# DLRM interaction and top layers on one core: the last two tables looked up whole, pairs in three chunks, layer 2's bias by a product, the sum's column turned by VectorE

## The chip, the cores and the metric

One of the cores of a Trainium2 chip runs the whole program. The metric is the device time of one execution in microseconds (us), lower is better. Engines in the text: TensorE (PE, with its weight loads as PEld), VectorE (DVE), ScalarE (ACT), GpSimd (POOL), SyncE (SP, which only issues transfers here).

## The reference

512 samples. Each has 26 embedding rows of 128 floats, picked by index out of 26 tables, and one dense row `r_bottom_output` of 128 floats. All 27 rows are multiplied with each other, and the 351 products of different rows go, with the dense row, through three layers:

```python
e = stack([tbl_f[ids[:, f]] for f in range(26)], axis=1)
all_emb = concatenate([bottom[:, None, :], e], axis=1)           # 512 x 27 x 128
gram = einsum('bfd,bgd->bfg', all_emb, all_emb)
z = gram[:, TRIU_I, TRIU_J]                                      # 512 x 351
h = concatenate([z, bottom], axis=1)                             # 512 x 479
h = maximum(h @ W_top1 + b_top1, 0)                              # 512 x 512
h = maximum(h @ W_top2 + b_top2, 0)                              # 512 x 256
y = h @ W_top3                                                   # 512 x 1
```

## The kernel before, in words

The samples stand in four tiles of 128 (`TILES`). Rows of 14 tables (`GATHERED`) come by indirect transfers that GpSimd issues, 56 of them, one for each tile and table (L348), and are turned on TensorE in four groups per tile, of 4, 4, 4 and 2 tables (step `turn`, L648), and copied to `emb` by ScalarE (L442). Rows of the other 12 tables (`LOOKED_UP`, each of 1000 or 1250 rows) are found by a product with a matrix of ones and zeros: VectorE writes `onehot` in 8 (for two tables 10) pieces of 128x512 (L518), ScalarE rounds the table to `hi`, VectorE takes the rest as `lo` (L501), and TensorE adds `hi` times `onehot` and `lo` times `onehot` (step `look`, L609), each in a first and a second half of the pieces.

The last two looked-up tables (numbers 10 and 11) are not looked up that way but in steps `part`: samples 0 to 255 first, samples 256 to 511 later, between the first `gram` steps, each with a moving operand of 256 columns (L636). ScalarE copies the sums of both tables to `emb` for each half of the samples (L434).

Behind that the steps of each tile t are: `gram` in four parts, each 32 small products (L671); VectorE and ScalarE copy one half of the products each to `gram` (L528, L451); VectorE turns them in 32x32 blocks in two instructions (L535, L536) and picks the 351 pairs to `z` (L543); `pairs`, TensorE turns `z` in three chunks of 117 (L679), ScalarE copies all three at once (L459) to `zt`; `bottom`, the dense part of layer 1 (L696), in two halves; `l1`, four steps of three products (L705), each step one block of 128 outputs over all chunks, and ScalarE's bias and maximum (L472); `l2` (L714), bias on VectorE (L549), and maximum, product with `W_top3` and sum in one instruction with a read of the accumulator (L551); `out`, a product with the identity turns the column of 128 sums into a row (L720), ScalarE copies it (L477), SP stores it (L328), in three stores for tiles 0, 1, and 2 and 3.

All engines run through one hand-written list, `ORDER` (L95 to L121), each doing its own share of a step; so a step's place in the list sets what every engine queues ahead of it. `turn`, `pairs`, `l2` and `out` share two PSUM banks (`ring`, `BANKS` = 2) in turn: a step waits on TensorE until the step two before it in that list has been copied out (`wait_emptied`, L556). `gram` uses three banks of `acc`, layer 1 three others. The products in f32 are two instructions each on TensorE; the rows count instructions.

## Time and profile before

| | |
|---|---|
| median of 3 runs | 107.57 us (107.38 to 110.34) |
| the profiled execution | 107.59 us |
| its span, first to last instruction | 105.9 us |
| TensorE busy | 98.3 us (93%), granted clock 0.999 |
| VectorE busy | 67.9 us (64%) |
| ScalarE busy | 53.2 us (50%) |
| GpSimd busy | 60.3 us (57%) |

The span is 1.7 us shorter than the execution's own time; what the change does is worked out inside the span and taken off the execution's time. "Busy" of TensorE is no measure of how fast it goes: instructions overlap, and the pace of a step is best read from start to start, or in the chain of work that ended last, where each piece is counted once.

### The profile page before, as it was taken

The numbers are of one execution on the slowest core, as the hardware profiler recorded it, in microseconds if no ns is written. First come the engines' busy times: TensorE is split into PE (matmuls) and PEld (weight loads), VectorE is DVE, ScalarE is ACT, GpSimd is POOL, SyncE is SP. The second block draws the span as 40 slices with busy tenths as digits, with TensorE's granted clock in tenths as the row PEclk, the third lists the DMA queues.
The fourth block names the chain that finished last, engine by engine and source line by source line (L and its number), as shares of the span: only waits on it lengthen the run. The fifth ranks groups of instructions, "written<-read, shape, count | busy, mean of one in ns | idle before, by whom it ended". The sixth has DMA issues, their size and how long they took to land.

```text
span 105.9 us, 3533 instructions
## 1 busy us (share of the span) xinstructions
PE 98.3 (93%) x1506; PEld 82.3 (78%) x1506; DVE 67.9 (64%) x157; ACT 53.2 (50%) x89; POOL 60.3 (57%) x65
## 2 busy tenths in 40 slices
PE   4999999999999999999769989999999989999971
PEld 4777777888888888888659979889888977996850
DVE  5499999999999999999940019108330833094021
ACT  3497659719939986984421324343153324222220
POOL 3777778877778877787777777777770000000000
PEclk9999999999999999999999999999999999999999
DMA  3899999658866845112699321222220000000000
GB/s 52 300 351 291 283 305 214 239 141 280 237 168 233 220 89 205 50 50 64 186 293 299 86 57 50 62 68 53 59 56 25 6 6 0 6 3 0 6 0 0
DMA packets 7460, 13.48 MB, mean 127 GB/s; under 512 B 1734, under 2 KB 3881, under 8 KB 7444
## 3 DMA queue, kind: packets, MB, share of 16 engines
q1 hardware_dynamic: 5340, 9.05, 28.0%
q0 software_dynamic: 1792, 3.67, 14.1%
q10 hardware_dynamic: 312, 0.52, 1.4%
q8 instruction: 12, 0.20, 0.7%
q14 instruction: 4, 0.03, 0.2%
HBM read 13.23 MB, written 0.01 MB: 125 GB/s over the span
## 4 chain that ended last, share of the span: by engine, by line
PE 47%; DVE 41%; issue 8%; ACT 1%; POOL 1%; POOLq 0%; DVEq 0%; ACTq 0%
DVE onehot L518 29%; PE acc L705 12%; PE acc L671 11%; DVE lo L501 11%; PE ring L714 7%; PE acc L636 6%; PE acc L696 4%; PE ring L648 3%; PE ring L679 2%; PE acc L573 2%; PE ring L720 1%; PE acc L587 1%; ACT far L379 1%; ACT zt L459 0%; DVE h L549 0%
## 5 line engine op out<-in xcount | busy, mean ns | idle before, releaser
L348 POOL DMA_INDIRECT rows<-tbl,ids_sb x56 | 59.5, 1062 | 18.3 <-issue 16.8
L518 DVE TENSOR_SCALAR onehot<-far 128x512 fp32r<-128x512 f32 x83 | 31.6, 437 | 1.3 <-ACT far L379 1.3
L609 PE MATMUL acc<-onehot,hi 128*128 128x512 f32 x84 | 23.8, 407 | 0.2 <-DVE onehot L518 0.2
L609 PE MATMUL acc<-onehot,lo 128*128 128x512 f32 x84 | 22.7, 393 | 0.0
L609 PEld LDWEIGHTS acc<-onehot,lo 128*128 128x128 f32 x84 | 15.8, 188 | 3.6
L609 PEld LDWEIGHTS acc<-onehot,hi 128*128 128x128 f32 x84 | 15.0, 191 | 4.3 <-DVE onehot L518 1.7
L528 DVE COPY gram<-acc 128x432 f32<-128x432 f32 x4 | 3.7, 917 | 22.3 <-PE acc L671 22.3
L365 ACT CAST hi<-raw 128x1024 fp32r<-128x1024 f32 (+1 forms) x11 | 12.0, 1088 | 10.7 <-issue 10.7
L501 DVE TENSOR_TENSOR lo<-raw,hi 128x512 fp32r<-128x512 f32 (+1 forms) x24 | 16.8, 702 | 0.0
L671 PEld LDWEIGHTS acc<-emb 128*27 128x27 f32 x1024 | 11.0, 104 | 4.1 <-issue 2.8
L671 PE MATMUL acc<-emb 128*27 128x27 f32 x1024 | 13.1, 192 | 1.1 <-issue 0.9
L705 PE MATMUL acc<-zt,w1z 117*128 117x128 f32 x96 | 12.6, 282 | 0.1
L705 PEld LDWEIGHTS acc<-zt,w1z 117*128 117x128 f32 x96 | 11.2, 191 | 0.7 <-ACT zt L459 0.3
L472 ACT ACTIVATE h<-acc,b_sb 128x128 f32<-128x128 f32 x16 | 5.0, 364 | 12.2 <-PE acc L705 12.2
L442 ACT COPY emb<-ring 128x512 f32<-128x512 f32 (+1 forms) x16 | 8.6, 546 | 3.7 <-PE ring L648 3.7
L451 ACT COPY gram<-acc 128x432 f32<-128x432 f32 x4 | 3.7, 930 | 11.0 <-PE acc L671 8.8
L648 PE MATMUL ring<-ident,rows 128*128 128x128 f32 x56 | 8.6, 272 | 0.4 <-issue 0.4
L549 DVE TENSOR_TENSOR h<-ring,b_b 128x256 f32<-128x256 f32 x4 | 1.7, 425 | 10.3 <-PE ring L714 10.3
L648 PEld LDWEIGHTS ring<-ident,rows 128*128 128x128 f32 x56 | 6.9, 141 | 1.5 <-issue 0.5
L714 PE MATMUL ring<-w_sb,h 128*128 128x256 f32 x32 | 7.9, 389 | 0.0
L636 PE MATMUL acc<-onehot,hi 128*128 128x256 f32 (+1 forms) x32 | 5.8, 303 | 1.2 <-DVE onehot L518 0.7
L714 PEld LDWEIGHTS ring<-w_sb,h 128*128 128x128 f32 x32 | 5.8, 190 | 0.9 <-issue 0.2
(45 smaller groups left out, 86.6 us busy)
## 6 DMA issues: line engine op xcount, KB each, us to landing
raw<-tbl SPq DMA_DIRECT2D x8, 448.0 KB
raw<-tbl SPq DMA_DIRECT2D x2, 576.0 KB
ids_b<-ids SPq DMA_DIRECT2D x4, 256.0 KB, 4.3
rows<-tbl,ids_sb POOLq DMA_INDIRECT x56, 3.7
w1z<-w SPq DMA_DIRECT2D x1, 702.0 KB
raw<-tbl SPq DMA_DIRECT2D x10, 52.0 KB
w_sb<-w SPq DMA_DIRECT2D x1, 512.0 KB
raw<-tbl ACTq DMA_DIRECT2D x1, 448.0 KB
```

The lines of the kernel that those rows point to most:

```text
L348: nc.gpsimd.indirect_dma_start(out=rows[:, t, slot, :], out_offset=None, in_=tables[table], in_offset=bass.IndirectOffsetOnAxis(ap=ids_sb[ ...
L365: nc.scalar.copy(hi[:, j % HL_RING, 0:chunks(j) * D], raw[:, j % RAW_RING, 0:chunks(j) * D]).then_inc(hi_ready, 2)
L442: nc.scalar.copy(emb[:, t, :, slots[0]:slots[0] + n], ring[:, b, 0:n * LANES].rearrange("d (p f) -> d p f", f=n)).then_inc(emb_turned, 1)
L472: nc.scalar.activation(h1[:, t % 2, m, :], acc[:, top_bank(2 * t + half), n * LANES:(n + 1) * LANES], ACT.Relu, bias=b1_sb[:, m:m + 1]).th ...
L501: nc.vector.tensor_tensor(lo[:, t % HL_RING, start:end], raw[:, t % RAW_RING, start:end], hi[:, t % HL_RING, start:end].bitcast(F32), ALU. ...
L518: ins = nc.vector.tensor_scalar(onehot[:, n % OH_RING, k, :], far[:, t % FAR_RING, :], row, None, ALU.is_equal)
L609: mm = nc.tensor.matmul(acc[:, look_bank(t), :], part_of[0:rows_of, t % HL_RING, c * D:(c + 1) * D], onehot[0:rows_of, n % OH_RING, k, :], ...
L636: mm = nc.tensor.matmul(acc[:, b, 0:PART], part_of[0:rows_of, t % HL_RING, c * D:(c + 1) * D], onehot[0:rows_of, n % OH_RING, k, samples * ...
L648: mm = nc.tensor.transpose(turn[:, :, n], rows[:, t, slot, :], ident[:])
L671: mm = nc.tensor.matmul(acc[QP * q:QP * q + NF, gram_bank(t, unit), k * NF:(k + 1) * NF], one, one, start=True, stop=True)
L705: mm = nc.tensor.matmul(acc[:, top_bank(2 * t + half), m * LANES:(m + 1) * LANES], w1z[:, c, part * 128:(part + 1) * 128], zt[:, t % 2, c, :],
L714: mm = nc.tensor.matmul(ring[:, b, 0:H2], h1[:, t % 2, k, :], w2_sb[:, k, :], start=(k == 0), stop=(k == M1 - 1))
```

## The change

- Tables 10 and 11 are looked up in steps `look` like the other ten; the steps `part` are gone. `turn` (2, 0) stands between the two. One copy for the samples of tile 0 and one for tiles 1 to 3 bring both tables to `emb` (semaphore `emb_last`).
- The order behind them is new. Layer 1 and layer 2 of tiles 0 to 2 all stand ahead of the four `gram` steps of tile 3.
- VectorE turns a tile's products in four instructions and picks `z` in three, one chunk of 117 at a time; `pairs` is a step for each chunk with a ring bank of its own and a copy of its own, and `l1` goes chunk by chunk (six steps, chunk c and half of the outputs).
- Layer 2's bias is added by a product of a matrix whose first row is ones with `b2_b`, ahead of the four others (step `l2`, part 0); VectorE's L549 is gone, and L551 reads PSUM. Tile 3's layer 2 has a bank of `acc` instead of a ring bank.
- The column of sums (now the first of 32 columns, the others zero) is turned by VectorE in 32x32 blocks; the steps `out`, with TensorE's product and ScalarE's copy, are gone. SP stores each tile by itself, as four pieces of 32 floats from four partitions.

```diff
+    behind = {2: (0, 0), 3: (0, 1), ..., 9: (1, 3), 10: (2, 0)}
+    for j in range(NL):
+        if j + 1 < NL:
+            order.append(("compare", j + 1, 0))
+        order.append(("look", j, 0))
+        if j in behind:
+            order.append(("turn", *behind[j]))
-    order += [("compare", NL - 1, 0), ("part", NL - 2, 0), ("part", NL - 2, 1), ("part", NL - 1, 0), ("part", NL - 1, 1),
-              ("turn", 2, 0),
...
+    order += [("bottom", 0, 0), ("gram", 0, 0), ("bottom", 0, 1), ("gram", 0, 1), ("turn", 2, 1), ("gram", 0, 2),
+              ("bottom", 1, 0), ("gram", 0, 3), ("turn", 2, 2), ("gram", 1, 0), ("gram", 1, 1), ("turn", 2, 3), ("gram", 1, 2),
+              ("pairs", 0, 0), ("pairs", 0, 1), ("gram", 1, 3), ("l1", 0, 0), ("pairs", 0, 2), ("l1", 0, 1), ("l1", 0, 2),
+              ("gram", 2, 0), ("l1", 0, 3), ("l1", 0, 4), ("gram", 2, 1), ("l1", 0, 5), ("bottom", 1, 1), ("gram", 2, 2),
+              ("pairs", 1, 0), ("pairs", 1, 1), ("gram", 2, 3), ("l1", 1, 0), ("pairs", 1, 2), *l1(1)[1:],
+              ("turn", 3, 0), ("bottom", 2, 0), *l2(0), ("turn", 3, 1), ("bottom", 2, 1),
+              ("pairs", 2, 0), ("pairs", 2, 1), ("l1", 2, 0), ("pairs", 2, 2), *l1(2)[1:], *l2(1), ("turn", 3, 2),
+              ("bottom", 3, 0), *l2(2), ("turn", 3, 3), *gram(3), ("l2", 3, 0), ("bottom", 3, 1),
+              ("pairs", 3, 0), ("l1", 3, 0), ("pairs", 3, 1), ("l1", 3, 1), ("pairs", 3, 2), ("l1", 3, 2), ("l1", 3, 3),
+              ("l1", 3, 4), ("l1", 3, 5), ("l2", 3, 1)]
-USES = [s for s in ORDER if s[0] in ("turn", "pairs", "l2", "out")]
+USES = [s for s in ORDER if s[0] in ("turn", "pairs") or s[0] == "l2" and s[1] < TILES - 1 and s[2] == 0]
...
+            for t in range(TILES):                                        # SP
+                sp.wait_ge(y_ready, t + 1)
+                sp.dma_start(out[t * LANES:(t + 1) * LANES, :].rearrange("(q u) o -> q (u o)", q=Q),
+                             y_row[0:LANES:QP, t, :]).then_inc(out_done, 16)
...
+                    if t == NL - 1:                                       # ScalarE, look
+                        act.wait_ge(oh_used, 2 * (t + 1))
+                        for a, e in ((0, 1), (1, TILES)):
+                            nc.scalar.copy(emb[:, a:e, :, first:first + n], ...).then_inc(emb_last, 1)
...
-                    act.wait_ge(pairs_done, t + 1)                        # ScalarE, pairs
-                    nc.scalar.copy(zt[:, t % 2, :, :], ...)
+                    act.wait_ge(pairs_done, ZC * t + part + 1)
+                    nc.scalar.copy(zt[:, t % 2, part, :], ring[0:ZK, bank(step, t, part), 0:LANES]
...
-                    nc.vector.transpose(pairs[:, 0:NF - 1, :], gram[:, t % 2, 1:NF, :]).then_inc(pairs_ready, 1)
-                    nc.vector.transpose(pairs[:, NF - 1:, :], gram[:, t % 2, 0:DELTAS, :]).then_inc(pairs_ready, 1)
-                    nc.vector.tensor_copy(z[:].rearrange("p (g e) -> p g e", g=NF), picked).then_inc(z_ready, 1)
+                    ends = [ZG * (c + 1) + DELTAS - 1 for c in range(ZC)]  # 21, 30, 39; WRAP is 26
+                    turn_pairs(0, ends[0], 1)
+                    pick_chunk(0, 1)
+                    turn_pairs(ends[0], WRAP, ends[0] + 1)
+                    turn_pairs(WRAP, ends[1], 0)
+                    pick_chunk(1, 3)
+                    turn_pairs(ends[1], ends[2], ends[1] - WRAP)
+                    pick_chunk(2, 4)
...
-                    nc.vector.tensor_tensor(h2[:, t % 2, :], ring[:, b, 0:H2], b2_b[:], ALU.add).then_inc(h2_ready, 1)
-                    nc.vector.scalar_tensor_tensor(h2w[:, t % 2, :], h2[:, t % 2, :], 0.0, w3_b[:], ALU.max, ALU.mult,
-                                                   accum_out=y_col[:, t:t + 1]).then_inc(y_summed, 1)
+                    nc.vector.scalar_tensor_tensor(h2w[:, t % 2, :], l2_out(t), 0.0, w3_b[:], ALU.max, ALU.mult,
+                                                   accum_out=y_col[:, t, 0:1]).then_inc(y_summed, 1)
+                    dve.wait_ge(y_summed, t + 1)
+                    nc.vector.transpose(y_row[:, t, :], y_col[:, t, :]).then_inc(y_ready, 1)
...
                 elif step == "gram":                                      # TensorE
-                        pe.wait_ge(emb_part, 1 if t < TILES // PARTS else 2)
+                        pe.wait_ge(emb_last, min(t + 1, 2))
                         pe.wait_ge(emb_turned, turn_count(t, TURNS - 1))
...
+                    if part == 0:                                         # TensorE, l2
+                        if t < TILES - 1:
+                            wait_emptied(step, t)
+                        else:
+                            pe.wait_ge(cut_dve, TILES - 1)
+                        nc.tensor.matmul(l2_out(t), ident[:, 0:1].broadcast_to([128, 128]), b2_b[:],
+                                         start=True, stop=False)
+                        continue
```

## Rows read from the trace of the kernel before

**Rows 1.** The page: the chain that ended last, shares of the span by engine, line.

```profile
PE 47%; DVE 41%; issue 8%; ACT 1%; POOL 1%; POOLq 0%; DVEq 0%; ACTq 0%
DVE onehot L518 29%; PE acc L705 12%; PE acc L671 11%; DVE lo L501 11%; PE ring L714 7%; PE acc L636 6%; PE acc L696 4%; PE ring L648 3%; PE ring L679 2%; PE acc L573 2%; PE ring L720 1%; PE acc L587 1%; ACT far L379 1%; ACT zt L459 0%; DVE h L549 0%
```

**Rows 2.** Stretches: length, busy time per engine (instructions), granted clock, DMA share, GB/s.

```profile
10.00:20.00 10.00, 10.00 (x45) 7.59 (x44) 10.00 (x26) 7.29 (x10) 7.90 (x7) 1.00 0.91 268
...
49.00:55.60 6.60, 5.14 (x38) 4.41 (x36) 5.10 (x12) 3.10 (x5) 5.31 (x5) 1.00 0.77 209
...
85.30:92.30 7.00, 6.96 (x282) 6.03 (x282) 1.24 (x4) 1.91 (x5) 0.00 (x0) 1.00 0.02 5
```

**Rows 3.** Timeline, 46 to 56 us: start, length, instruction, and idle time before it.

```profile
46.93 1.07 PE L609 MATMUL acc<-onehot,hi 128*128 128x512 f32 x4
...
51.54 0.71 PE L636 MATMUL acc<-onehot,hi 128*128 128x256 f32 x4 [0.47 <-ACT emb L422]
...
53.55 0.74 PE L636 MATMUL acc<-onehot,hi 128*128 128x256 f32 x4 [0.71 <-DVE onehot L518]
...
54.93 0.62 ACT L434 COPY emb<-acc 128x512 f32<-128x512 f32 x1 [3.48 <-PE acc L636]
...
55.65 0.73 PE L671 MATMUL acc<-emb 128*27 128x27 f32 x64 [0.32 <-issue]
```

**Rows 4.** The chain that ended last, in order of time: start, length, instructions.

```profile
1.55 1.65 PE acc L573 x6
...
54.89 0.44 PE ring L648 x4
...
56.38 1.15 PE acc L636 x8
57.53 0.67 PE acc L671 x51
...
86.06 1.92 PE ring L714 x8
...
93.85 0.89 PE acc L696 x8
...
97.43 2.94 PE acc L705 x24
```

**Rows 5.** Timeline, tile 3 behind its last gram step.

```profile
92.44 0.91 DVE L528 COPY gram<-acc 128x432 f32<-128x432 f32 x1 [3.53 <-PE acc L671]
93.38 1.04 DVE L535 STREAM_TRANSPOSE pairs<-gram 128x832 f32<-128x832 f32 x1
...
94.35 0.57 DVE L536 STREAM_TRANSPOSE pairs<-gram 128x416 f32<-128x416 f32 x1
...
94.95 0.78 DVE L543 COPY z<-pairs 128x351 f32<-128x351 f32 x1
...
96.89 0.48 ACT L459 COPY zt<-ring 117x384 f32<-117x384 f32 x1 [2.30 <-PE ring L679]
...
102.64 0.42 DVE L549 TENSOR_TENSOR h<-ring,b_b 128x256 f32<-128x256 f32 x1 [5.24 <-PE ring L714]
103.10 0.42 DVE L551 SCALAR_TENSOR_TENSOR h2w<-h,w_b 128x256 f32<-128x256 f32 x1
...
104.10 0.26 ACT L477 COPY y<-ring 1x128 f32<-1x128 f32 x1 [2.85 <-PE ring L720]
```

**Rows 6.** Timeline, 69 to 86 us: a short copy, and two gram steps.

```profile
69.11 0.40 ACT L442 COPY emb<-ring 128x256 f32<-128x256 f32 x1
...
70.83 0.97 PE L671 MATMUL acc<-emb 128*27 128x27 f32 x64
...
85.33 0.73 PE L671 MATMUL acc<-emb 128*27 128x27 f32 x64 [0.43 <-issue]
```

**Rows 7.** DMA of 0 to 63.2 us: GpSimd's queue, packets, MB, share (32 packets a gather).

```profile
q0 software_dynamic: 1344, 2.76, 17.7%
```

**Rows 8.** Waits of SP's queue: in total, times, longest.

```profile
SPq L183 <- DMA out<-y: 0.9, 1, 0.9
```

206 lines of the change are left out of this document (80 added, 126 removed).

## The prediction

> **What bounds the kernel now.** I read the chain that ended last first [rows 1]: VectorE carries 41% of the span and TensorE 47%. Taken with the stretches [rows 2] this means two stages, one after the other. Up to 53.5 us VectorE writes ones and zeros without a pause (10.00 of 10.00 us busy at 10 to 20 us), with TensorE just behind it. From then on TensorE is the bound: between 85.3 and 92.3 us it is busy 6.96 of 7.00 us. At the end there is a third stage, a tail in which one tile has nothing beside it: the last gram step's products are copied from 92.44 us, and the output copy ends at 104.36 us (104.10 and 0.26) [rows 5]. The change touches the seam of the first two stages, the amount and order of TensorE's work in the second, and each link of the tail. I count in time from 48.9 us, where TensorE takes up table 10 in both kernels; ahead of that the instructions are the same but for one clear of 128x128 on VectorE while it still waits for its first input, which I cost at 0 (0.2 us if that wait is not there).
>
> **The seam: whole looks for parts.** A part step's eight instructions of 256 columns take 1.15 us in the chain [rows 4], 0.144 each; there are 64 in eight steps, 9.2 us. A whole look has 16 of 512 columns. Four of them take 0.91 us from start to start (46.93 to 47.84, the group shown in [rows 3] and the next one), 0.228 each, so 32 take 7.3 us: 1.9 us less TensorE work. Beside that, TensorE now waits 0.47 us for a copy that frees banks (the change's looks 10 and 11 have banks of their own, so it is gone) and 0.71 us for VectorE's last pieces [rows 3]. With whole looks TensorE is late, not early: 48.95 and 3.65 us for table 10, 0.44 for `turn` (2, 0), 3.65 for table 11 is 56.7 us, while VectorE's last pieces are there at 53.5 as before [rows 3] and its last `lo` about half a microsecond behind. So that wait goes too, and TensorE becomes the bound 4.6 us earlier than now. Behind it the copy of tile 0's samples (128x256, near the 0.40 of [rows 6]) takes the place of one of 0.62 us, and `bottom` (0, 0) covers it: 0.2 us of wait before the first gram step instead of 0.32.
>
> **TensorE's work up to the last gram step.** Prices of the steps, all from the chain [rows 4]: gram 0.67 us; a turned table 0.11 (four in 0.44); a half of bottom 0.445; a tile's layer 1 3.07 with its starts (2.94 for tile 3's 24 instructions); a layer 2 1.92; and 0.24 for one instruction of 128x256, so 0.48 for the bias product. A chunk of pairs is 0.11.
> Before, from 48.9 to 92.3: parts 9.2, 28 turned tables 3.1, 16 gram steps 10.7, six halves of bottom 2.7, three tiles' pairs 1.0, two and a half layers 1 7.7, two layers 2 3.8, one out 0.2. That is 38.4 of 43.4 us; 5.0 are waits and slow steps. 1.9 of them are those named (0.47, 0.71, 0.32, and the 0.43 before `gram` (3, 0), where the table turned just before had to be copied first [rows 6]). The rest, 3.1, is spread: gram steps that last 0.97 rather than 0.74 us [rows 6] (the 11% of [rows 1] are 11.7 us where sixteen clean ones are 10.7, and gaps inside them come on top), and layer 1 waiting for one copy of three chunks.
> After, for the same point: looks 7.3, turned tables 3.1, gram 10.7, seven halves of bottom 3.1, nine chunks 1.0, three layers 1 9.2, three layers 2 with their bias 7.2. That is 41.6 us. More work stands ahead of the last gram step, because layer 1 and 2 of tile 2 have moved there; the bias products (1.4 us for three) take part of what the whole looks save. New waits that I can place: 0.2 before the first gram step; `turn` (2, 3) wants gather 42 at 63.1 us, whose packets are all there by 63.2 (1344 is 42 times 32 [rows 7]) with its semaphore a little behind, 0.4; in tile 2 the third and second chunk wait for ScalarE's copies, 0.4; and `gram` (3, 0) stands right behind `turn` (3, 3) and its copy of 0.40, 0.6 us with nothing between. With 1.6 us of these the last gram step would end at 92.2. The slow steps stay: I add 1.5 us, as the grams alone show about 1.3. Result 93.7 us against 92.3, 1.4 us later; bounds 0.0 later (no slow steps) and 3.1 later (all that is spread now stays).
>
> **The tail, to the end of layer 2.** Now 10.3 us, from 92.3 (the copy behind it starts at 92.44) to 102.6 (L549 starts at 102.64): VectorE's copy and both turns and the pick end at 95.73 (94.95 and 0.78), TensorE and ScalarE bring `zt` at 97.37 [rows 5], layer 1 starts at 97.43 and takes 2.94 [rows 4], layer 2 ends 2.25 behind it. In the new order the first chunk needs 21 of the 39 blocks: by the two turns, 1.04 us for 26 blocks and 0.57 for 13, a block is 0.036 and the start 0.09, so 0.86. The pick of a third is between 0.26 (0.78 shared out) and 0.36 (with a start of 0.1), taken as 0.33. So chunk 0 of `z` is there 2.2 us behind the copy's start, not 3.3. One transposition and its way to ScalarE is 0.4, a copy of 128 columns about 0.3 (0.48 for three times as much, 0.40 for twice [rows 5, 6]). Layer 1 starts 3.0 us behind 92.44 where it is 5.0 now. The other two chunks follow at 1.0 and 1.8 us behind the first and layer 1 needs 1.0 for each chunk, so they stay just ahead of it; two more transpositions stand inside it, 0.2. Layer 1 and so layer 2 end 1.8 us earlier, 8.5 us behind the last gram step. Bounds: 1.3 (each chunk costs TensorE a wait of 0.25) and 2.2. Layer 2's bias product and `bottom` (3, 1) lie in the gap behind the last gram step, 0.9 of its 2.9 us, and cost nothing; without that gap they would be 0.9.
>
> **The end.** From 102.64 to 104.36 now, 1.72 us: bias, maximum and sum, product, copy [rows 5]. After: L551 alone with its accumulator read, 0.43, a wait of 0.04 and a turn of one block, 0.13 by the line above: 0.6. That is 1.1 us less, near certain; at worst L551 out of PSUM is slower by 0.1. The store has four pieces of 128 bytes where it now has one row. SP's wait for its last store is 0.9 us [rows 8]; no row shows pieces so short, so between 0 and 0.5 more, taken as 0.1, since the wait is a round trip and not bytes. The Trainium skill, DMA: Bandwidth & Descriptors (Specifications), says that below 512 B a transfer is done as read-modify-write; by that the store should be the slower one, and the value would be the upper end. The first three stores and the fourth issue on SP lie beside other work.
>
> **Sum.** +1.4 -1.8 -1.1 +0.1 = -1.4 us: 107.59 - 1.4 = 106.2 us, against a median of 107.57 which is the profiled execution's own time to 0.02 us.
>
> **Rivals.**
> First, more gain (104.9 us and less). The slow gram steps are there where weights and gathers crowd the queues and where TensorE has just waited; if the chance waits of the new order (0.4 for a gather, 0.6 for a copy) fall on them rather than behind them, 1 to 1.5 us of the 3.1 added are not there. For it: the slow steps are irregular, 0.97 beside many of 0.73. Against it: they don't follow the waits visibly.
> Second, the order eats the gain (107.3 us). The last gram step comes 2.6 us later, not 1.4, since two layers stand ahead of it and four gram steps stand in a row, 256 short products without a long one to hide behind; the tail gives 1.5 back. For it: TensorE is 6.96 of 7.00 busy there already [rows 2], so anything put ahead counts in full. Against: 41.6 us of work is a sum of steady prices.
> Third, the other side: TensorE's clock. In the tail TensorE will stand for 1.4 us behind `bottom` (3, 1) and 0.5 us more before layer 1, after four gram steps with a 0.6 us wait ahead of them; before layer 2 of the last tile it never idles so long now, and the granted clock is 1.00 in each stretch shown [rows 2]. If it fell to 1.2 GHz there, layer 1 and 2 of tile 3, 2.94 and 1.94 us, would take twice as long: 106.2 + 4.9 = 111 us. It decides from the point where the idle time in the tail is long enough to lower the grant. The six products at the very start take 0.27 us each in the chain [rows 4] where the same shape takes 0.11 later, which is what such a fall looks like. The Trainium skill, TensorE: Matmul & The Clock Gate (The HAM clock gate), says that an idle array falls back to 1.2 GHz. Against it: idle times of 0.47 and 0.71 us within three microseconds [rows 3] left the grant at 1.00 [rows 2].
> That the change does not do what it says: looks whole could be no cheaper if VectorE still ended last; but it ends near 54 and TensorE at 56.7 by the sum, so at most the 1.9 us are 1.2, which is inside the bounds.
>
> **Chances.** About 2% (2.15 us) is what a measurement of this kernel tells from no change. The forecast, 105.5 to 106.9: 0.45. More gain, 103.9 to 105.4: 0.28. Gain eaten, 107 to 108.2: 0.19. Clock, 111: 0.06; slower in another way: 0.02. So faster by over 2% 0.28, within 2% 0.64, slower by over 2% 0.08. The range runs from 104.0 to 108.1 and leaves out the clock and the ends of the other cases.
>
> **What the profile would show.** The last L609 near 56.7 us and the first gram step near 57.3. VectorE idle from 54 to about 62. The last gram step's end at 93.7 (92.3 to 95.4). Between it and layer 2's end 8.5 us, with the first `zt` copy near 2.6 us behind VectorE's copy's start. From layer 2's end to VectorE's last turn 0.65 us. The granted clock at 1.00 in the tail. I am wrong on the order if the last gram step ends past 95; on the chunks if layer 1 of tile 3 shows gaps over 0.2 us between chunks; on the bias if layer 2 lasts other than 2.4 us; on the clock if layer 1 of tile 3 takes over 4 us.

## The result and the profile after

The changed kernel takes 115.31 us (113.39 to 116.17, 4 runs) where the kernel before takes 108.72 us beside it (107.38 to 110.34, 4 runs). The ratio is 1.062, with a 95% interval of 1.033 to 1.091: slower, by 6 to 7 us. Executions of one kernel fall into faster and slower ones, and the ratio compares the faster ones alone (113.39 and 114.84 against 107.38 and 107.57), while the profiled execution of the changed kernel, 115.77 us, is not one of them. It has a span of 114.0; its TensorE clock was 0.955 on average, where it was 0.999 before. The four runs' mean clocks lie between 0.94 and 0.985. The run of 113.39 us has 0.985 over 111.6 us: an estimate from these two numbers is 3.4 us granted 0.50, and so at most 1.7 us lost to the clock. It is 5.8 us slower than the kernel before, so in that run the clock is the smaller part of the loss.

Where the time went can be read in five views. First the page of the changed kernel: the granted clock in 40 slices, and the chain that ended last, by engine.

```profile
PEclk9999999999999999999999998599999999975599
...
PE 82%; issue 6%; DMA 4%; ACT 3%; DVE 2%; SPq 0%; DVEq 0%; ACTq 0%
```

VectorE's 41% of [rows 1] have become 2%: TensorE carries the chain from the first looks to the end, as forecast. But two groups of digits in the clock's line are below 9 (the 8 and 5, then the 7, 5 and 5), which the line of before doesn't have, and 6% of the chain is "issue", time in which TensorE waited for nothing that the profile names. The windows, with columns as in [rows 2], put both into the second half:

```profile
58.00:63.00 5.00, 4.97 (x260) 4.22 (x245) 0.00 (x0) 1.78 (x3) 3.78 (x5) 1.00 0.26 68
63.00:68.00 5.00, 3.19 (x198) 2.68 (x196) 3.74 (x8) 1.68 (x3) 3.78 (x5) 1.00 0.25 59
68.00:73.00 5.00, 3.58 (x76) 3.20 (x76) 2.08 (x4) 0.79 (x4) 3.78 (x5) 0.76 0.22 57
...
99.00:103.00 4.00, 2.37 (x91) 1.98 (x90) 2.02 (x3) 0.00 (x0) 0.00 (x0) 0.79 0.02 4
103.00:107.00 4.00, 3.33 (x14) 3.07 (x15) 1.64 (x6) 0.74 (x3) 0.00 (x0) 0.50 0.00 0
107.00:111.00 4.00, 3.93 (x23) 3.48 (x22) 0.00 (x0) 1.20 (x5) 0.00 (x0) 0.86 0.00 0
```

TensorE is busy 3.19 and 3.58 of 5 us in two stretches of a stage in which it is the bound. The order matters: the stretch with the idle time comes first at a clock of 1.00, and the lower clock comes behind it. The timeline of TensorE at the first place (start, length, instruction, idle time before it):

```profile
56.10 1.09 PE L627 MATMUL acc<-onehot,lo 128*128 128x512 f32 x4
...
57.72 0.73 PE L658 MATMUL acc<-emb 128*27 128x27 f32 x64
...
63.26 0.86 PE L658 MATMUL acc<-emb 128*27 128x27 f32 x67
65.74 0.81 PE L658 MATMUL acc<-emb 128*27 128x27 f32 x61 [1.62 <-issue]
66.48 0.44 PE L638 MATMUL ring<-ident,rows 128*128 128x128 f32 x2
66.85 0.96 PE L658 MATMUL acc<-emb 128*27 128x27 f32 x64
69.42 0.47 PE L665 MATMUL ring<-ident,z 128*117 128x128 f32 x2 [1.61 <-issue]
```

The looks end at 57.19 and the first gram step starts at 57.72 ([rows 3, 4]: the first gram step starts at 55.65 there, with half of the part steps still to come). Behind each x stands a count of TensorE's product instructions, called records here; a product in f32 is two of them, and a gram step's 32 products are 64. Six microseconds on, TensorE stands for 1.62 us three records into a gram step (the row with 67 runs into the next step). The program has no wait at that place. Between that stall and the next lie 61, 2 and 64 records, 127 in all. The second stall stands where TensorE takes up `pairs` (0, 0), where the program does wait: the chain has a copy of ScalarE end at 68.08, so up to 0.27 of its 1.61 us can be that wait. And tile 3, from its gram steps to the end:

```profile
95.97 1.83 PE L658 MATMUL acc<-emb 128*27 128x27 f32 x171 [0.53 <-issue]
...
99.88 0.91 PE L658 MATMUL acc<-emb 128*27 128x27 f32 x85 [2.08 <-issue]
...
100.91 0.90 DVE L531 COPY gram<-acc 128x432 f32<-128x432 f32 x1 [4.90 <-PE acc L658]
...
101.85 0.88 DVE L540 STREAM_TRANSPOSE pairs<-gram 128x672 f32<-128x672 f32 x1
102.76 0.35 DVE L550 COPY z<-pairs 128x117 f32<-128x117 f32 x1
...
103.88 0.27 ACT L465 COPY zt<-ring 117x128 f32<-117x128 f32 x1 [5.47 <-PE ring L665]
104.20 1.22 PE L689 MATMUL acc<-zt,w1z 117*128 117x128 f32 x4 [0.41 <-ACT zt L465]
...
106.49 2.74 PE L689 MATMUL acc<-zt,w1z 117*128 117x128 f32 x16
...
109.31 1.99 PE L708 MATMUL acc<-w_sb,h 128*128 128x256 f32 x8
...
111.41 0.42 DVE L570 SCALAR_TENSOR_TENSOR h2w<-acc,w_b 128x256 f32<-128x256 f32 x1 [6.70 <-PE acc L708]
...
111.87 0.21 DVE L573 STREAM_TRANSPOSE y_row<-y_col 128x32 f32<-128x32 f32 x1
```

The four gram steps have become 171 records, 2.08 us of nothing, and 85 records. Behind it the 24 records of layer 1 take 5.03 us (104.20 to 109.23, granted 0.50 up to 107 us and 0.86 behind) where 24 took 2.94 [rows 4]. The end behind layer 2 is short now: 111.41 to 112.08 is 0.67 us where it was 1.72 [rows 5].

Last, the DMA view. It has a queue that the prediction did not look at. The rows are its packets, megabytes and share, first of the kernel before between 58 and 91 us, then of the changed kernel, of the whole span and of the single microseconds 97 to 98 and 100 to 101:

```profile
q8 instruction: 9, 0.15, 1.7%
```

```profile
q8 instruction: 11, 0.18, 0.6%
...
q8 instruction: 1, 0.02, 6.3%
...
q8 instruction: 1, 0.02, 7.0%
```

Instructions themselves come by DMA, in packets of 16 KB. In the kernel before nine of them fall in 33 us, one each 3.7 us. In the changed kernel the packet that begins between 97 and 98 us ends within the stall of 97.80 to 99.88, and none begins in 98 to 100: the next starts behind the stall. Each of the three long stalls ends 1.3 to 1.5 us behind the end of such a packet, by the packets' own times in the trace (64.4, 67.9 and 98.35 against 65.74, 69.42 and 99.88).

So the 7.1 us by which the last gram step ends later than forecast (100.8 against 93.7) are for the most part 4.9 us in three long stalls (1.62 + 1.61 + 2.08, less the 0.4 that the forecast had for a gather near there) and up to 1.7 us at a lowered clock (0.24 of the 5 us from 68, and 0.10 of the 5 from 73, where the granted clock was 0.90); some 0.5 us I can't place. Some 1.7 us more are lost in tile 3's layer 1 by the clock (5.03 us, where the same steps took 3.29 at 1.00 in two runs below).

### The profile page after: what moved, and what is told of

Same layout as the page of the kernel before. It is cut to its first block, busy times and chain, and to the rows that moved or that the text cites. A ratio compares the mean times of both kernels' runs of the same rounds, so it can differ in the third digit from the quotient of the medians.

```text
span 114.0 us, 3504 instructions
## 1 busy us (share of the span) xinstructions
PE 101.6 (89%) x1474; PEld 85.2 (75%) x1474; DVE 69.0 (61%) x174; ACT 53.4 (47%) x93; POOL 60.5 (53%) x65
## 4 chain that ended last, share of the span: by engine, by line
PE 82%; issue 6%; DMA 4%; ACT 3%; DVE 2%; SPq 0%; DVEq 0%; ACTq 0%
PE acc L627 41%; PE acc L689 13%; PE acc L658 10%; PE ring L638 5%; PE ring L708 5%; DMA raw<-tbl 4%; PE acc L679 3%; PE ring L665 2%; PE acc L708 2%; PE ring L703 1%; ACT gram L458 1%; DVE gram L531 1%; DVE pairs L540 1%; ACT emb L449 1%; ACT hi L368 1%
## 5 line engine op out<-in xcount | busy, mean ns | idle before, releaser
L627 PE MATMUL acc<-onehot,hi 128*128 128x512 f32 x100 | 28.2, 405 | 0.6 <-ACT hi L368 0.6
L627 PE MATMUL acc<-onehot,lo 128*128 128x512 f32 x100 | 27.0, 393 | 0.0
L627 PEld LDWEIGHTS acc<-onehot,lo 128*128 128x128 f32 x100 | 18.8, 188 | 4.3
L627 PEld LDWEIGHTS acc<-onehot,hi 128*128 128x128 f32 x100 | 17.6, 188 | 5.2 <-DVE onehot L521 2.2
L689 PE MATMUL acc<-zt,w1z 117*128 117x128 f32 x96 | 16.1, 324 | 0.4 <-ACT zt L465 0.4
L689 PEld LDWEIGHTS acc<-zt,w1z 117*128 117x128 f32 x96 | 14.6, 233 | 1.0 <-ACT zt L465 0.7
L465 ACT COPY zt<-ring 117x128 f32<-117x128 f32 x12 | 3.0, 266 | 13.9 <-PE ring L665 13.5
L570 DVE SCALAR_TENSOR_TENSOR h2w<-ring,w_b 128x256 f32<-128x256 f32 x3 | 1.3, 425 | 10.5 <-PE ring L708 10.5
L540 DVE STREAM_TRANSPOSE pairs<-gram 128x672 f32<-128x672 f32 (+3 forms) x16 | 7.5, 487 | 0.1
L665 PE MATMUL ring<-ident,z 128*117 128x128 f32 x12 | 3.9, 353 | 2.7 <-issue 1.6
```

The source lines that it names most:

```text
L540: nc.vector.transpose(pairs[:, start:end, :], gram[:, t % 2, first:first + end - start, :]).then_inc(pairs_ready, 1)
L627: mm = nc.tensor.matmul(acc[:, look_bank(t), :], part_of[0:rows_of, t % HL_RING, c * D:(c + 1) * D], onehot[0:rows_of, n % OH_RING, k, :], ...
L665: nc.tensor.transpose(ring[0:ZK, bank(step, t, part), 0:LANES], z[:, part * ZK:(part + 1) * ZK], ident[:]).then_inc(pairs_done, 1)
L689: mm = nc.tensor.matmul(acc[:, top_bank(2 * t + half), n * LANES:(n + 1) * LANES], w1z[:, c, m * 128:(m + 1) * 128], zt[:, t % 2, c, :], s ...
```

## The experiments

Two theories. *Fetch*: TensorE's instructions arrive in blocks, two of them come 3.4 us apart at the closest in this trace (63.48 and 66.91; 3.3 in all the traces here), and a dense row of gram steps (128 instructions in 0.67 us each) eats blocks faster than that; the clock falls afterwards, because TensorE stood. *Data*: the products wait for an operand or a bank that the trace doesn't name. A third, *clock first*, has the lower grant as the cause and the stalls as its look.

On the chips of the first, second and fifth group of runs every kernel, the unchanged one too, took some 40 us more, nearly all before the first gram step (told under what was not expected). Of those runs only the trace behind the first gram step is read. A time "from the first gram step to the end" is used for that: 48.71 us in the kernel before, 54.36 in the changed one.

### Is it the density of small instructions?

`e1_fill3` puts four long products between the second and third gram step of tile 3, `e2_fillall` six more near the other two stalls.

```diff
-    *gram(3),
+    *gram(3)[:2], ("fill", 3, 4), *gram(3)[2:],
...
+    elif step == "fill":
+        for n in range(part):
+            nc.tensor.matmul(acc[:, 2 if t == 3 else 4, 256:512], ident[:], bot[:, 0:256],
+                             start=(t == 3), stop=(t == 3))
```

> The changed kernel with four extra products of 128x256 in f32 (8 instruction pairs, 1.9 us of TensorE time by the 0.24 us of such an instruction) between gram (3, 1) and gram (3, 2), written to a bank that is free there. Theory (refill): TensorE runs out of instructions; between two boundaries 256 instructions apart it needs 3.7 us at least (stalls end at 65.74, 69.42 and 99.88 us, each 3.7 us behind the last boundary by count), and four gram steps in a row want two such blocks in 2.7 us. Then the extra work fills the stall of 2.08 us: the stall shrinks to under 0.4 us, the last gram step ends within 0.3 us of where it does now, and since TensorE does not stand, the granted clock stays 1.00 behind it: layer 1 and 2 of tile 3 run 1.5 to 2 us faster, so the whole is 1.5 to 2.5 us faster than the changed kernel. Rival (data): the stall is a wait for a copy or a gather that no row names; then it goes as well, but so it would with any delay. Rival (work): TensorE is simply short of time; then the extra work adds 1.9 us. Rival (clock by itself): the clock falls as before, 0.63 at 100 to 105 us.

> As the one before, and three such products behind gram (1, 0) and three ahead of gram (1, 2), 2.9 us of extra TensorE work in all where it stalls 1.62 and 1.34 us and where the clock then falls to 0.66. Theory (refill): both stalls shrink to under 0.5 us together, the granted clock is 1.00 all the way, and against the run with one filling the time is 1 us less to 0.5 us more, though 2.9 us of work were added. Rival (work or data): 1.3 to 2.9 us more than the run with one filling.

Measured: 157.80 and 157.27 us against 148.96 (with the disturbance). The timeline of `e1_fill3`, tile 3's gram steps:

```profile
138.32 1.44 PE L658 MATMUL acc<-emb 128*27 128x27 f32 x128 [0.53 <-issue]
139.69 1.99 PE L671 MATMUL acc<-bot,ident 128*128 128x256 f32 x8
141.62 1.27 PE L658 MATMUL acc<-emb 128*27 128x27 f32 x128
```

The stall of 2.08 us is gone. With 1.9 us of useless work in them the four steps take 4.57 us (138.32 to 142.89) where they took 4.82 (95.97 to 100.79). The stalls of tiles 0 and 1, whose surroundings were left alone, stayed (1.66 and 2.21 us). In `e2_fillall` the longest stall with no releaser behind the first gram step is 0.90 us (under 0.5 for two together was expected), and the clock reads 1.00 from 102 to 122 us. In the traces the work put in cost next to nothing, since it filled time that would have passed anyway; the changed kernel was not run on this chip, so no pair of times shows it. The clock of the tail was still below 1 in both, against the expectation: it falls there without a stall.

### Is it the place in the instruction stream?

`e3_shift` adds 32 products of one element early (128 instructions with their weight loads) and leaves the rest as it is. If an operand is late, the stall stays at the same product. If it is a block's edge, it moves.

```diff
+    for n in range(32):
+        nc.tensor.matmul(acc[0:1, look_bank(0), 0:1], ident[:, 0:1], ident[:, 0:1], start=True, stop=True)
```

> The changed kernel with 128 tiny TensorE instructions (32 products of one by one, about 1.6 us, at 5 us where TensorE waits for VectorE anyway), so that every later instruction has a count 128 higher. Theory (refill): the long stall in tile 3's gram steps moves from behind about 171 products to behind about 107 (64 pairs earlier) and stays near 2 us, since four steps hold a whole block wherever it begins; the first long stall moves from within gram (1, 0)'s end to about one gram step earlier. Time within 1.5 us of the changed kernel. Rival (data): what a stall waits for does not know the count: the stalls stay where they are, behind the same products.

Measured: 178.66 us against 148.96, and the timeline of tile 3's gram steps:

```profile
158.53 2.35 PE L660 MATMUL acc<-emb 128*27 128x27 f32 x235 [0.53 <-issue]
...
162.59 0.35 PE L660 MATMUL acc<-emb 128*27 128x27 f32 x21 [1.71 <-issue]
```

The stall stands behind the 235th record of tile 3's gram steps and no longer behind the 171st. That is not the place expected, 107; but 107 and 235 are 128 records apart, about one block: at 107 lies the edge before, for which the block had come in time. In tiles 0 and 1 the stalls moved as expected, 64 records towards the start, a product record and its weight load being two of the 128 instructions added: the one behind gram record 323 stands behind 259 now (0.69 us), the one behind 448 stands behind 385, one record into a step (2.10 us). Counted over the whole stream, these two have not moved. The windows end just before TensorE resumes and count its records up to there (behind the first x), first in the changed kernel, then in `e3_shift`:

```profile
0.00:65.70 65.70, 61.89 (x589) 49.87 (x590) 54.19 (x135) 40.92 (x57) 50.03 (x54) 1.00 0.64 191
0.00:69.40 69.40, 63.96 (x716) 51.69 (x717) 55.40 (x138) 42.08 (x59) 52.81 (x57) 1.00 0.62 184
0.00:99.80 99.80, 91.71 (x1348) 76.69 (x1349) 64.69 (x163) 51.44 (x86) 60.47 (x65) 0.98 0.46 135
```

```profile
0.00:125.10 125.10, 74.32 (x589) 57.63 (x590) 52.37 (x132) 40.88 (x57) 56.47 (x65) 0.80 0.36 107
0.00:128.90 128.90, 76.06 (x717) 59.07 (x717) 54.70 (x138) 42.01 (x59) 56.47 (x65) 0.80 0.35 104
```

The same counts return in kernels with other work at these places:

| kernel | records ahead of a stall with no releaser (its length, us) |
|---|---|
| changed kernel | 589 (1.62), 716 (1.61), 1348 (2.08) |
| `e3_shift` | 462 (0.42), 589 (0.69), 717 (2.10), 844 (1.94), 1476 (1.71) |
| `g0_before`, below | 716 (0.81) |
| `g6_before_looks`, below | 335 (2.40), 462 (1.67), 716 (0.68) |

Within a kernel they are one, two or five times 126 to 128 records apart. The instruction packets follow the same count: in the kernel before TensorE passes nine such places from record 335 to 1349, and by the packets' own times nine packets begin, each 0.2 to 2.0 us behind one of them. With that *data* falls: what a stall waits for goes by the count of instructions, whatever products stand there. In total `e3_shift` takes 21 us more than `e1_fill3` beside it; the added records account for 5 of them (6.0 to 11.3 us in the trace, 64 records), and the rest, on a chip in the disturbance told below, I have not explained.

The Trainium skill, Runtime: NRT & Kernel Launch (Instruction fetch mechanics), says that instructions come in blocks of 256 and that crossing a block's edge is mostly hidden. The 127 records between two stalls (254 instructions with their weight loads) and the shift agree with the 256; "mostly hidden" holds for the kernel before, and not for the changed one, whose dense stretches stand for 1.6 to 2.1 us at an edge.

### Spread the gram steps

`e4_spread3`, and `e4b_spread3` on another chip, move only tile 3's gram steps and their neighbours: each now has a layer 2 or a bottom step beside it, as in the order before.

```diff
-    *l2(1), ("turn", 3, 2), ("bottom", 3, 0), *l2(2), ("turn", 3, 3), *gram(3), ("l2", 3, 0), ("bottom", 3, 1),
+    ("turn", 3, 2), ("turn", 3, 3), ("l2", 1, 0), ("gram", 3, 0), ("l2", 1, 1), ("gram", 3, 1), ("bottom", 3, 0),
+    ("l2", 2, 0), ("gram", 3, 2), ("l2", 2, 1), ("gram", 3, 3), ("l2", 3, 0), ("bottom", 3, 1),
```

> The changed kernel with the list reordered for tile 3 alone: its four gram steps stand between layer 2's steps of tiles 1 and 2 (gram, layer 2 of tile 1, gram, bottom and bias, gram, layer 2 of tile 2, gram). Same instructions, same work. Theory (refill): 256 instructions now last 3.6 us or more there; no stall over 0.5 us behind 90 us, the granted clock stays at 1.00 in the tail, and the time falls by 3 to 4 us (2.1 of stall, 0.5 of wait for a copy, 1.5 to 2 of clock). Rival (clock by itself): the stall goes but the clock falls as before: 2 to 2.5 us less. Rival (the tail's own length, the order eats the gain): TensorE's work ahead of the last gram step is the same, so the time stays within 1 us.

> The same kernel as e4_spread3 once more, on another chip if there is one: the first job's chip ran every kernel some 40 us longer while the gathers ran. Expected as then: no stall in tile 3's gram steps, granted clock 1.00 in the tail, 3 to 4 us less than the changed kernel's 115 us where that ran, so 111 to 112 us against 107.6 to 108.7 of the kernel before.

Measured: 154.01 and 155.12 us against 148.96 and 149.29; the changed kernel did not run beside them, so the 3 to 4 us expected can't be read from the times. Timeline of `e4_spread3`, and its window over the tail:

```profile
131.81 0.74 PE L659 MATMUL acc<-emb 128*27 128x27 f32 x64
132.48 1.99 PE L709 MATMUL ring<-w_sb,h 128*128 128x256 f32 x8
134.41 0.74 PE L659 MATMUL acc<-emb 128*27 128x27 f32 x64
...
143.93 2.05 PE L690 MATMUL acc<-zt,w1z 117*128 117x128 f32 x16
```

```profile
136.00:146.00 10.00, 8.18 (x171) 6.82 (x169) 4.31 (x11) 1.31 (x6) 0.00 (x0) 1.00 0.01 2
```

No stall, gram steps of 0.74 us, and layer 1 of tile 3 from 142.69 to 145.98, 3.29 us where it was 5.03 in the changed kernel: the clock stayed at 1.00, although TensorE waits 1.39 us for VectorE there. The two stalls in tiles 0 and 1 stayed, 1.45 and 1.67 us.

It would be wrong to read from this that the stall ahead is what lowers the clock of the tail. `e4b_spread3`, the same kernel, has no stall there either and the same wait of 1.39 us, and its clock falls: layer 1 of tile 3 takes 4.89 us. `g1_after`, below, has the stall (1.77 us) and keeps its clock: 3.29 us. Their windows over that layer:

```profile
147.00:151.00 4.00, 4.00 (x22) 3.95 (x22) 0.00 (x0) 1.11 (x4) 0.00 (x0) 0.57 0.00 0
```

```profile
103.00:107.00 4.00, 3.93 (x30) 3.61 (x31) 0.49 (x2) 1.68 (x6) 0.00 (x0) 1.00 0.00 0
```

All of these have the wait of 1.0 to 1.4 us for the first chunk of `z`. Behind it the clock falls in some runs and not in others; what decides was not found.

`e7_reorder` and `e7b_reorder` do the same to the whole list behind the looks: the changed kernel with an order in which no more than two gram steps stand together, and those rarely.

```diff
-    ("gram", 0, 0), ("bottom", 0, 1), ("gram", 0, 1), ("turn", 2, 1), ("gram", 0, 2), ("bottom", 1, 0), ("gram", 0, 3), ...
+    ("gram", 0, 0), ("gram", 0, 1), ("bottom", 0, 0), ("turn", 2, 1), ("bottom", 0, 1), ("gram", 0, 2), ...
+    ("l2", 0, 0), ("bottom", 2, 0), ("gram", 2, 0), ("l2", 0, 1), ("pairs", 1, 0), ("gram", 2, 1), ("l1", 1, 0), ...
+    ("l2", 1, 0), ("gram", 3, 0), ("pairs", 2, 0), ("l2", 1, 1), ("bottom", 3, 0), ("gram", 3, 1), ("l1", 2, 0), ...
```

> The changed kernel with nothing changed but the order of the list behind table 11: no more than two gram steps stand without a longer step between them but once, and the pairs, layer 1 and layer 2 steps of each tile lie between the gram steps of the next. Theory (refill): with 256 instructions never wanted in much less than 3.6 us, the stalls go (0.4 us left) and the clock stays; what the prediction had counted on comes back, and more, as TensorE no longer waits for the last tile's first chunk: 3 to 4 us faster than the kernel before. Rival (the parts of the change themselves are dear: whole looks, chunks, bias products): still slower than the kernel before by 2 us or more, since all of them are in it.

> The changed kernel with the new order once more, now that a job has met a chip on which the kernel before takes 107.5 us. By the pair without gathers (g3 against g0, and g3 against g1) 2 us slower than the kernel before and 5 to 6 us faster than the changed kernel: 109 to 110.5 us. By the theory that the order alone was at fault it would be faster than the kernel before.

Measured: 150.61 against 149.29 us, and 150.00 against 150.52. The idle times with no releaser are 0.53 us in the one and 0.53 and 0.85 in the other (the 0.53 stands before the first gram step); beside them TensorE waits 1.80 us for VectorE's first chunk of `z` in both. As times they miss both expectations, faster than the kernel before and 109 to 110.5 us, on disturbed chips. From the first gram step to the end 44.99 and 45.36 us where the changed kernel has 54.36 and the kernel before 48.71; these were not on one chip, and which part of the difference the chips make is left open here and asked again below.

### The two other parts alone

`e5_before_looks` is the kernel before with only the whole looks, `e6_before_end` with only the new bias and end (four bias products), `f7_end3` the same with the bias product for tile 3 alone.

```diff
 e5_before_looks
-    ("part", 10, 0), ("part", 10, 1), ("part", 11, 0), ("part", 11, 1), ("turn", 2, 0), ("gram", 0, 0), ("part", 10, 2), ...
+    ("look", 10, 0), ("turn", 2, 0), ("look", 11, 0), ("gram", 0, 0), ("gram", 0, 1), ("gram", 0, 2), ("turn", 2, 1), ...
 f7_end3
-    ("l2", 2, 0), ("pairs", 3, 0), ("l1", 3, 0), ..., ("l2", 3, 0), ("out", 3, 0)
+    ("l2", 2, 0), ("pairs", 3, 0), ("bias", 3, 0), ("l1", 3, 0), ..., ("l2", 3, 0)
```

> The kernel before with one part of the change alone: tables 10 and 11 looked up whole, one copy for tile 0 and one for the rest; the eight part steps are gone, and so are the four that stood between the gram steps of tile 0, which now follow one another with only turn (2, 1) between. Theory (refill): 1.9 us of TensorE work and 1.2 us of its waits are saved, but the gram steps of tile 0 lose what stood between them: 256 instructions in under 2 us, where a refill takes some 3.6. I expect stalls of 1.5 and 1.0 us and one of 1.3 within the gram steps of tiles 0 and 1, the clock maybe down behind them, and a whole of -0.5 to +1.5 us against the kernel before. Rival (work): the saved work shows in full, 2.5 to 3 us faster.

> The kernel before with the other end alone: bias by a product for all four tiles, maximum and sum out of PSUM, the column turned by VectorE, four stores. All theories agree on 1.1 us less behind layer 2 (measured in the changed kernel: 0.67 us from the start of L570 to the end of the turn, against 1.72) and on 1.9 us more TensorE work for the four bias products less 0.9 for the products with the identity: 0 to 0.5 us faster if TensorE's work counts in full, 1 us faster if some of it lies in waits, slower by up to 0.5 if the clock or the refills come in.

> As g7_end3 with the gathers, so a kernel that computes all of the reference: the kernel before, its end turned by VectorE, the bias by a product for tile 3 alone. On a chip where the kernel before takes 107.5 us: 105.5 to 106.5 us, 1 to 2% faster than it.

Measured: 151.52 and 152.20 us against 149.29, and 149.07 against 150.52. The ranges (144 to 158, 139 to 156, 135 to 153) are wider than any effect asked about: these three settle nothing as times. In the traces the stretch from first gram step to end is 46.89 us in `e5_before_looks`, with stalls of 1.17 and 1.68 us (1.5, 1.0 and 1.3 were expected), 48.29 in `e6_before_end` and 46.45 in `f7_end3`.

### The same without gathers

To be rid of the disturbance, the g kernels load the gathered rows with plain transfers of SP, 16 of them, from one table in place of 56 indirect ones. All else is as in the kernel named.

```diff
-    nc.gpsimd.indirect_dma_start(out=rows[:, t, slot, :], in_=tables[table], in_offset=...).then_inc(rows_in[t][g], 16)
+    sp.dma_start(rows[:, t, slots[0]:slots[0] + k, :]..., tables[3][0:KP * k, :]...).then_inc(rows_in[t][g], 16)
```

> The kernel before without GpSimd's 56 gathers: the rows of the 14 gathered tables are taken instead by 16 plain loads of SP, one for each tile and group, from rows of one table (the rows are not those asked for, all else is computed on them). On the chips of the first two jobs every kernel stood for some 40 us while the gathers ran; this takes the gathers away from all that are compared here. If the gathers are what stood in the way, this is back near the 107.6 us of the kernel before where it ran undisturbed, 105 to 109 us. Layer 2 of tile 3 ends 53 to 54 us behind the start of table 10, as there.

> The changed kernel, likewise without the gathers. Theory (refill): the stalls are all there (1.6 and 1.4 to 2 us in tiles 0 and 1, 2 us in tile 3), and the clock falls behind them: 4 to 8 us slower than g0_before. Rival (gathers: TensorE waits for rows that come late, or their packets delay its instructions): without them the stalls are gone, and the changed kernel is at the forecast, 1 to 2 us faster than g0_before.

> The changed kernel with tile 3's gram steps spread (as e4_spread3), without the gathers. Theory (refill, and the clock behind a stall): 3 to 4 us faster than g1_after, no stall behind the first 15 us after the looks. Clock by itself: 2 us.

> The changed kernel with the whole list behind table 11 in the new order (as e7_reorder), without the gathers. Theory (refill): 1 to 3 us faster than g0_before and 7 to 10 us faster than g1_after, all with the parts of the change in it. Rival (the parts themselves are dear): slower than g0_before.

Measured, all four on one chip:

| kernel | us | first gram step | last ends | end | stalls in this stage |
|---|---|---|---|---|---|
| g0_before | 105.06 (104.78 to 105.53) | 54.33 | 89.96 | 102.00 | 0.32, 0.81, 0.43 |
| g1_after | 112.74 (112.15 to 114.78) | 57.18 | 99.61 | 108.96 | 1.73, 2.20, 0.53, 1.77 |
| g2_spread3 | 111.09 (110.29 to 113.21) | 57.48 | 98.86 | 109.53 | 2.00, 1.40 |
| g3_reorder | 107.28 (106.75 to 107.46) | 57.24 | 92.01 | 103.79 | 0.53, 1.12 |

The change costs 7.7 us without gathers too (112.74 less 105.06), so neither they nor their semaphores are the cause; and the stalls stand behind the same records, 589, 716 and 1348. Timeline of `g1_after`:

```profile
65.08 0.71 PE L655 MATMUL acc<-emb 128*27 128x27 f32 x61 [1.73 <-issue]
...
69.02 0.47 PE L662 MATMUL ring<-ident,z 128*117 128x128 f32 x2 [2.20 <-issue]
...
98.70 0.91 PE L655 MATMUL acc<-emb 128*27 128x27 f32 x85 [1.77 <-issue]
```

The same work in another order, `g3_reorder`, takes 5.5 us less. That is the price of the order, measured: with ranges that lie 4.7 us apart at their nearest. Spreading tile 3 alone gives 1.7 us, with ranges that overlap, where 3 to 4 were expected. `g2_spread3` kept its first stalls; its traced run is the longest of the five (113.21 us), with a clock of 0.50 at 67 to 72 us, so its row stands for that run and not for the median.

What stays is 2.2 us of `g3_reorder` over `g0_before`, where 1 to 3 us faster was expected: here the rival, that the parts of the change are dear themselves, came true. The first gram step starts 2.9 us later, and the stage behind it is only 1.1 us shorter (46.55 against 47.67), though half of the part steps are out of it. How this divides among the whole looks, the chunks and the four bias products (1.9 us of TensorE work) no run separates. What the trace shows is a hole: with the part steps gone from between the gram steps of tile 0, and no tile's `z` ready, TensorE waits 1.80 us for VectorE. The window of `g3_reorder` over it:

```profile
62.00:67.00 5.00, 3.20 (x81) 2.60 (x76) 3.68 (x8) 1.48 (x4) 0.00 (x0) 0.75 0.02 3
```

VectorE is busy 3.68 us there, TensorE 3.20. The clock is lowered behind this wait too (0.75), and here it is a wait for data.

Then the parts alone, on another chip, where the kernel before (with its gathers) took 107.51 us (106.78 to 109.25) and `g0_before` was not run: `g5_before_end`, `g6_before_looks`, `g7_end3` and `g8_fillall`, the counterparts of e6, e5, f7 and of e2.

> The kernel before with the other end alone (bias by a product for all four tiles, L551 out of PSUM, column turned by VectorE, a store per tile), without the gathers, against g0_before at 105.1 us. All theories: 1.1 us less behind layer 2; four bias products are 1.9 us more TensorE work less 0.9 for the products with the identity. I expect 104.5 to 105.5 us. If this is over 106, the bias products cost more than their 0.48 us each.

> The kernel before with whole looks alone, without the gathers: tile 0's gram steps lose the part steps between them. Theory (refill, clock): stalls over 1 us among the gram steps of tiles 0 and 1 and a lower clock behind them; 106 to 108.5 us, 1 to 3.5 us slower than g0_before, although 1.9 us of TensorE work is gone. Rival (the order of tile 3 and of the later layers is the whole of it): 103 to 104.5 us.

> The kernel before with the other end, but the bias by a product for tile 3 alone (placed where TensorE waits for the copy of that tile's pairs; VectorE adds it for tiles 0 to 2 as before), without the gathers. 1.1 us less behind layer 2, 0.7 us less TensorE work for three products with the identity ahead of it: 103 to 104 us, 1 to 2 us faster than g0_before. If it is not faster than g5_before_end, the bias products were hidden in waits.

> The changed kernel with ten extra products (4.8 us of TensorE work, as e2_fillall) among the dense gram steps, without the gathers, against g1_after at 112.7 us. Theory (refill): the extra work takes the place of stalls: 111.5 to 114 us, with no stall over 1 us in the trace and the clock at 1.00 up to the tail. Rival (TensorE short of time, or a wait for data that would be paid besides): 116 to 117.5 us.

Measured: 106.58 (105.36 to 109.22), 109.44 (106.80 to 110.58), 105.82 (105.14 to 108.36) and 112.92 (111.72 to 113.83) us. Against what was expected, `g5_before_end` is above 106 us, `g7_end3` some 2 us above its forecast and above the 105.06 of `g0_before` on the other chip, `g6_before_looks` a little above its range, and `g8_fillall` within it. The whole looks by themselves are the slowest of the three parts, 2.9 and 3.6 us over the two neighbours by the medians. But the four runs of `g6_before_looks` are 106.80, 108.65, 110.24 and 110.58 us, at mean clocks of 1.00, 0.984, 0.969 and 0.982, and the lowest is 1.4 and 1.7 us over the neighbours' lowest: as a time the price of the whole looks is not settled closer than that. The traced run is the one of 110.24 us. Its timeline and window show the mechanism at its barest, since here three gram steps of tile 0 stand in a row with no other step between. By the order of the changed kernel one would have looked for the stall a block later; it stands 89 records behind the first gram step's start already (335 from the start of the kernel):

```profile
60.80 1.08 PE L674 MATMUL acc<-emb 128*27 128x27 f32 x103 [2.40 <-issue]
...
64.64 0.76 PE L674 MATMUL acc<-emb 128*27 128x27 f32 x44 [1.67 <-issue]
```

```profile
62.00:67.00 5.00, 3.33 (x76) 2.90 (x76) 1.53 (x2) 0.89 (x2) 0.00 (x0) 0.53 0.01 3
```

Two stalls, 2.40 and 1.67 us. From the end of the one to the end of the other, 60.80 to 64.64, it is 3.84 us for 127 records (103, 4 and 20); the clock, 1.00 up to the end of the first, reads 0.53 behind it. `g0_before`, with the part steps between the gram steps, has no wait behind records 335 and 462: those steps had been what gave the fetch its time.

`g8_fillall` takes 4.8 us of filler products and comes out at `g1_after`'s time, 112.92 to 112.74 (another chip, so to within what chips differ by). Its worst stall is 0.63 us, behind record 589 again, and its clock over the stretch that reads 0.53 above is 1.00:

```profile
62.00:67.00 5.00, 4.37 (x144) 3.46 (x144) 3.70 (x8) 1.42 (x3) 0.00 (x0) 1.00 0.02 7
```

This speaks against *clock first*: nothing was done to the clock, only TensorE was kept at work. And in the changed kernel the stalls that end at 65.74 and 69.42 us both lie in time granted 1.00 (the window 0.00:69.40 above). The Trainium skill, TensorE: Matmul & The Clock Gate (The HAM clock gate), has an idle array fall to 1.2 GHz, and the 0.50 to 0.53 of these windows, which is that level, stand behind idle times as it says. These need not be stalls: the tail of `g8_fillall`, with a wait of 1.40 us for VectorE and no stall, read 0.67.

The new end, last: `g7_end3` has the layer 2 of tile 3 summed and turned in

```profile
101.48 0.42 DVE L551 SCALAR_TENSOR_TENSOR h2w<-ring,w_b 128x256 f32<-128x256 f32 x1 [5.02 <-PE ring L723]
...
101.95 0.21 DVE L554 STREAM_TRANSPOSE y_row<-y_col 128x32 f32<-128x32 f32 x1
```

0.68 us. From first gram step to end it has 47.34 us, `g5_before_end` 47.97 and `g0_before`, on the other chip, 47.67. So of the 1.05 us that the short end wins, 0.7 are lost again with one bias product, and all of it with four, by one trace each; with gathers, where the kernel before has 48.71, the same two ends have 46.45 and 48.29, so these differences are not firm. The one waits for the ring bank and holds layer 1 up (it starts at 96.27, layer 1 at 96.80, 0.7 us behind the copy of `zt`). The ratio of `g7_end3` to the kernel before, 0.983 (0.974 to 0.992), is not a gain, as it has no gathers. No version was shown to beat the kernel before on the whole computation.

## Why the prediction was wrong, point by point

The forecast was 106.2 us and the chance of slower by over 2% 0.08; the kernel came out at 115.31, 9 us above.

- *The seam: right.* Looks end at 57.2 (forecast 56.7), first gram step at 57.7 (57.3), VectorE done at 53.7. The looks' price held.
- *Named waits: right in size.* `gram` (3, 0) waits 0.53 us for the copy (0.6). Between chunks of layer 1 the gaps stay small.
- *The step that failed: "The slow steps stay: I add 1.5 us".* I had 3.1 us "spread" in the kernel before and took the part that I saw in the gram steps over as it stood, though these were the very rows that the new order touches. They had two causes. Some were small hits at block edges: behind records 716 and 1097 of the kernel before TensorE loses 0.3 us each, kept small because parts, layers and turned tables stood between the gram steps. With two to four gram steps in a row such hits became 1.6 to 2.1 us each. Others were not at an edge: the step of 0.97 us in [rows 6] loses its time behind record 812, and in `g0_before`, without gathers, the same step takes 0.74. That fits what the first rival said of gathers. The term was +1.4 us for the last gram step (2.6 in the second rival, 3.1 at the bound) and measured +8.5.
- *"Against: 41.6 us of work is a sum of steady prices"*, by which I held the second rival down, is the same error. The rival named the place exactly, "four gram steps stand in a row, 256 short products without a long one to hide behind", and was priced at 1.2 us, for want of a mechanism. 0.67 us was the price of a gram step among others, not of a gram step.
- *The third rival, the clock*, came true in part: in the traced run the clock fell at 68 to 78 us, which I had not foreseen, and in tile 3's layer 1 (5.03 us, against 3.29 with the clock at 1.00). I had it wait on TensorE's idle time behind `bottom` (3, 1). In this trace it was already down behind the stall before (0.79 at 99 to 103 us), but `e4b_spread3` and `g8_fillall` show it fall behind that idle time with no stall ahead, so the rival's mechanism is real; it strikes in some runs. I put 0.06 on it and took the waits of [rows 3] for proof against; they are less than half as long as the stalls. It is not the main cause: by the estimate above it costs 1.7 us at most in the run of 113.39.
- *The tail by chunks: right, and overrun by the clock in the traced run.* The first `zt` copy starts 2.97 us behind VectorE's copy (forecast 2.6; VectorE's turn and pick are each within 0.02 of it, TensorE's transposition is slower at the low clock). From last gram step to layer 2's end it takes 10.5 us where 8.5 was forecast. In `g1_after`, where the clock holds, it is 8.6 (99.61 to 108.17).
- *The end: right.* 0.67 us for 0.6; the turn of one block costs 0.21, not 0.13.

Together: +8.5 for the order and its stalls (4.9 of stalls and up to 1.7 of clock over forecast, the +1.4 that was foreseen, and 0.5 not placed), +0.2 where -1.8 stood for the tail (that is the clock), -1.05 for the end and +0.4 for the four-piece store (1.9 us from the last turn to the span's end where 1.5 lay behind the last copy; forecast +0.1, bound 0.5): +8.05, against 8.1 between the spans, 114.0 and 105.9.

What stays open: what sets the pace of the blocks, and at which instruction the next is asked for, which decides whether the first edge of a dense stretch is passed without a stall (`e3_shift`) or not (`g6_before_looks`); how the lost time splits exactly between stalls and clock; why the clock falls in the tail in some runs and not in others; how the 2.2 us of `g3_reorder` over `g0_before` divide; and whether the kernel before with the new end and its bias by VectorE would be faster.

## What to carry to other kernels

TensorE has a price in instructions besides that in columns: a stretch of short products that runs through some 127 records (with their weight loads 254 instructions) faster than in some 3.5 us can stand at a block's edge; instruction packets never came closer than 3.3 us here. In such a kernel put long products between the short ones, even when the order looks worse for data; a "filler" that is real work is best, and removing one can cost what it saves. When rows of one kind have uneven durations without a wait, find out at which instruction number they fall before carrying them over as a constant.

## What the runs showed that I had not expected

The fetch itself: TensorE stalls marked only "issue", at fixed places in the instruction stream, 1.6 to 2.4 us long, which the DMA view gives away by a queue named "instruction".

On four of the chips every kernel with gathers took 40 to 55 us more, the unchanged one too (149.0, 149.3, 150.5 and 160.4 us). In the traces of that group most of it is lost before the first gram step, while GpSimd issues its gathers. TensorE's timeline of `e1_fill3` there:

```profile
50.10 0.27 PE L638 MATMUL ring<-ident,rows 128*128 128x128 f32 x1 [0.80 <-issue]
50.82 0.32 PE L638 MATMUL ring<-ident,rows 128*128 128x128 f32 x1 [0.45 <-issue]
51.53 0.33 PE L638 MATMUL ring<-ident,rows 128*128 128x128 f32 x1 [0.39 <-issue]
```

Records of which four otherwise take 0.44 us together start 0.7 us apart. Without gathers, on the chip where the kernel before took 160.4 us, the same kernel took 105.06. So the gathers have to do with it, but how was not found; the kernels were compared behind that stretch, or without gathers.
